# Second layer's attention: folded weights, a scale on GpSimd, heads summed in PSUM, unrolled by tiles

## What is computed

```
scores[h] = (X Wq[h] + bq[h]) (X Wk[h] + bk[h])^T / sqrt(128)
p[h]      = softmax(scores[h])
h         = h + sum over heads of p[h] (X Wv[h] + bv[h]) Wo[h]
```

## Time and profile before

| | us |
|---|---|
| median of three runs | 3473.49 |
| lowest, highest | 3467.41, 3475.90 |
| profiled execution, its own time | 3499.97 |
| its span | 3498.2 |

### The profile page before, as it was taken

One profiled execution on the slowest core, in us unless ns is written; L12 is line 12 of the kernel. 1 busy time (PEld: TensorE's weight loads), 2 busy tenths in 40 slices (PEclk: granted clock), 3 DMA queues, 4 the chain that ended last, 5 costly groups with the idle time before them and its releaser, 6 DMA issues.

```text
span 3498.2 us, 57433 instructions
## 1 busy us (share of the span) xinstructions
PE 3053.3 (87%) x18996; PEld 2673.3 (76%) x19032; DVE 2413.0 (69%) x4368; ACT 1801.3 (51%) x3135; POOL 1773.0 (51%) x1524
## 2 busy tenths in 40 slices
PE   1556666668999999879999999999799999999997
PEld 1434445457788888759999999999699999999986
DVE  1456766643677676657777777777577777777774
ACT  0256666523666565525555555555455555555544
POOL 5466656500200000126666666666366666666663
PEclk9879999969999999979999999999899999999997
DMA  1010000000000000010000000000000000000010
GB/s 41 32 25 18 19 13 18 7 25 21 13 0 0 0 0 0 11 50 28 27 27 27 27 27 27 27 27 28 17 28 27 27 27 27 27 27 27 27 34 7
DMA packets 36972, 75.92 MB, mean 22 GB/s; under 512 B 9644, under 2 KB 13876, under 8 KB 36120
## 3 DMA queue, kind: packets, MB, share of 16 engines
q1 hardware_dynamic: 35352, 71.68, 6.5%
q0 software_dynamic: 1536, 3.15, 0.3%
HBM read 65.36 MB, written 1.05 MB: 19 GB/s over the span
## 4 chain that ended last, share of the span: by engine, by line
PE 47%; issue 5%; POOL 3%; DVE 1%; ACT 0%; POOLq 0%; DVEq 0%; ACTq 0%
PE lat_ps_h L1837 19%; PE lat_ps_z L1851 9%; PE lat_ps_s L1763 7%; PE lat_ps_t L1790 6%; PE lat_ps_z L1781 3%; POOL lat_zz L1570 2%; PE lat_ps_z L1773 2%; PE lat_ps_z L1861 1%; POOL latm_wq L1549 0%; POOL latm_wq L1543 0%; POOL latm_att L1562 0%; POOL latm_vcg L1554 0%; PE lat_ps_s L1879 0%; DVE latm_norm L1669 0%; DVE latm_h L1675 0%
## 5 line engine op out<-in xcount | busy, mean ns | idle before, releaser
L1837 PE MATMUL lat_ps_h<-latm_share,latm_attT 100*128 100x256 f32 x6144 | 886.8, 286 | 0.1
L1837 PEld LDWEIGHTS lat_ps_h<-latm_share,latm_attT 100*128 100x128 f32 x6144 | 818.7, 189 | 24.9 <-DVE latm_attT L1626 11.8
L1562 POOL TENSOR_TENSOR latm_att<-latm_sc,latm_tot 128x400 f32<-128x400 f32 x516 | 441.3, 855 | 617.7 <-DVE latm_tot L1621 588.1
L1570 POOL TENSOR_TENSOR lat_zz<-lat_zz,lat_zsq 128x512 f32<-128x512 f32 x514 | 660.3, 1285 | 0.3
L1698 ACT ACTIVATE latm_sc<-latm_sc 128x400 f32<-128x400 f32 x516 | 279.1, 541 | 430.8 <-DVE latm_sc L1612 430.8
L1851 PE MATMUL lat_ps_z<-latm_attT,latm_vg 100*128 100x512 f32 x1536 | 485.8, 424 | 0.0
L1619 DVE TENSOR_REDUCE latm_tot<-latm_sc 128x4 f32<-128x400 f32 x516 | 291.3, 565 | 157.4 <-ACT latm_sc L1698 157.4
L533 POOL TENSOR_TENSOR ret_probs<-ret_probs,ret_shared 128x1024 f32<-128x1024 f32 x128 | 305.7, 2389 | 181.4 <-ACT ret_probs L666 181.4
L1626 DVE TENSOR_TENSOR latm_attT<-lat_ps_t,latm_attT 100x512 fp32r<-100x512 f32 x514 | 349.8, 681 | 61.7 <-ACT latm_attT L1714 61.7
L1714 ACT CAST latm_attT<-lat_ps_t 100x512 fp32r<-100x512 f32 x514 | 301.0, 586 | 147.3 <-PE lat_ps_t L1790 123.1
L1763 PE MATMUL lat_ps_s<-latm_wk,lat_xr 128*128 128x400 f32 x1548 | 368.8, 347 | 3.0 <-issue 3.0
(11 more groups left out here) (339 smaller groups left out, 5012.4 us busy)
## 6 DMA issues: line engine op xcount, KB each, us to landing
lat_w_in<-in_w_quads SPq DMA_DIRECT2D x65, 512.0 KB, 3.6
lat_wq_in<-in_wq_quads SPq DMA_DIRECT2D x65, 256.0 KB, 2.6
ret_qk_head<-ret_qk_parts SPq DMA_DIRECT2D x256, 32.0 KB, 2.0
moe_w<-in_W SPq DMA_DIRECT2D x2, 1024.0 KB
mha_wqk<-in_Wqk SPq DMA_DIRECT2D x1, 1152.0 KB, 5.6
ret_shared<-in_xpos_q SPq DMA_DIRECT2D x1, 1024.0 KB, 5.3
ret_shared<-in_xpos_k SPq DMA_DIRECT2D x1, 1024.0 KB, 5.0
latw_wkv<-in_Wkv SPq DMA_DIRECT2D x1, 1024.0 KB
```

The source lines that it names most:

```text
L1562: nc.gpsimd.tensor_tensor(att[:, u].rearrange("p (j l) -> p j l", j=QH), sc[:, u].rearrange("p (j l) -> p j l", j=QH), tot[:, u].unsqueeze ...
L1570: nc.gpsimd.tensor_tensor(zz[:, t], zz[:, t], zsq[:, u], ALU.add).then_inc(s["zz_added"], 1)
L1837: mm = e.matmul(ps_h[:, t, :], attT[:, t % 2, a_part, j * P:(j + 1) * P], share[:, u, w_part, j * FF2:(j + 1) * FF2], start=False, stop=Fa ...
```

## The change

Before the loop, the two weights of a head are multiplied once (`fold`): Wq[h] Wk[h]^T as `wqk` and Wv[h] Wo[h] as `wvo`, each 128 x 128 for a head. `keys` of a unit are then X times `wqk` plus a bias column `bqk`, and the scores are X itself (`xr`, already split) against `keys`: no q is made. The values are X times `wvo` plus `bvo`, so that p times them is already the head's share of the output, and `output` goes.

To take the biases in, POOL and DVE centre the query and key weights over the model width, with a bias column added, and X carries +1 (`lift`). These steps stand in front of and inside the norm (`means`, `fold`, `fold_bias`).

The heads of one sequence now come one after the other (n = 8 * sequence + head), and `gather` adds all 8 heads into the same two banks of `psO`; once for each sequence and half the sum is copied, turned back and added to h. Since heads are summed there, the division must come before: DVE's `invert` makes 1/sum of each tile (128x1), and GpSimd multiplies the tile's 128x1024 probabilities by it (`normed`), after the exponential and ahead of the transposes.

All is written out in 128 steps, one a tile, with no hardware loop. On PE every step holds the same parts: 6 matmuls of `gather` for tile step-7 on, 8 transposes of tile step-2, 6 matmuls of the scores of tile step+2, and in two steps of eight 3 matmuls of the next keys, in two others 4 of the next values, both into `psT[:, 0]`. `probs` has four buffers instead of three.

The weight transfers are seven instead of five, 2.0 MB in all instead of 2.8 MB.

```diff
@@ -103,9 +103,12 @@
-    def __init__(self, core, h, ident, xT, psT, l2=False, xr=None, room=None):
+    def __init__(self, core, h, ident, xT, psT, l2=False, xr=None, room=None, lift=None):
...
+        if meanwhile is not None:
+            meanwhile()
...
+                nc.scalar.activation(self.xr[:, 0, g * BANK:(g + 1) * BANK], src, ACT.Identity, bias=self.rise[:]).then_inc(self.high, 1)
...
@@ -947,244 +866,345 @@
+        makes_keys = lambda step: (step // TB + 1, step % TB // 2 - 1) if step < K - TB and step % TB in (2, 4) else None
+        makes_values = lambda step: ((step + 2) // TB, (step + 2) % TB // 2) if TB <= step + 2 < K and (step + 2) % TB in (0, 2) else None
...
-            with e.Fori(0, H) as hh:
-                for b in range(B):
-                    n = hh * B + b
-                    if b == 1:
-                        e.wait_ge(k_ready, START + n + 1)
-                        head_weights(hh + 1)
-                    low_values(n + 1)
+            nc.gpsimd.tensor_copy(bv_wide[:], bv[:].unsqueeze(2).to_broadcast([P, H, P])).then_inc(s["bv_widened"], 1)
+            e.wait_ge(s["qk_mean"], START + 2)
+            nc.gpsimd.tensor_tensor(wqT[:], wqT[:], wide(mean[:, 0]), ALU.add).then_inc(s["q_centred"], 1)
+            nc.gpsimd.tensor_tensor(wkT[:], wkT[:], wide(mean[:, 1]), ALU.add).then_inc(s["k_centred"], 1)
+            def low_values(n, half):
+                e.wait_ge(s["v_high"], START + 2 * n + half + 1)
+                nc.gpsimd.tensor_tensor(v[:, n % 2, 1, chunk(half)], v_full[:, chunk(half)], v[:, n % 2, 0, chunk(half)].bitcast(F32),
+                                        ALU.subtract).then_inc(s["v_ready"], 1)
+            low_values(0, 0)
+            low_values(0, 1)
+            for step in range(K):
+                e.wait_ge(s["inv_ready"], START + step + 1)
+                nc.gpsimd.tensor_scalar(probs[:, step % 4], probs[:, step % 4], inv[:, step % TB:step % TB + 1], None, ALU.mult
+                                        ).then_inc(s["normed"], 1)
+                if step >= 1 and makes_values(step - 1):
+                    low_values(*makes_values(step - 1))
...
+            def fold():
+                e.wait_ge(s["q_centred"], START + 1)
+                e.wait_ge(s["bv_widened"], START + 1)
+                for j in range(H):
+                    mm = e.matmul(psO[:, j // 4, j % 4 * D:(j % 4 + 1) * D], bv_wide[:, j], wo[:, j], start=True, stop=True)
+                mm.then_inc(s["folded"], 1)
+                for j in range(H):
+                    mm = e.matmul(psS[:, 1, j // 4, j % 4 * D:(j % 4 + 1) * D], wvT[:, j], wo[:, j], start=True, stop=True)
+                mm.then_inc(s["folded"], 1)
+                e.wait_ge(s["k_centred"], START + 1)
+                for j in range(H):
+                    mm = e.matmul(psS[:, 0, j // 4, j % 4 * D:(j % 4 + 1) * D], wkT[:, j], wqT[:, j], start=True, stop=True)
+                mm.then_inc(s["folded"], 1)
+            def fold_bias():
+                e.wait_ge(norm.xT_ready, START + NT // 4)
+                for j in range(H):
+                    mm = e.matmul(psT[:, 0, j:j + 1], wqT[:, j], bk[:, j:j + 1], start=True, stop=True)
+                mm.then_inc(s["folded"], 1)
+            def make_keys(n, c, dst):
+                for j, (w_part, x_part) in enumerate(PARTS):
+                    mm = e.matmul(dst, wqk[:, w_part, head_of(n % H)], xr[:, x_part, n // H * S + c * BANK:n // H * S + (c + 1) * BANK],
+                                  start=(j == 0), stop=(j == 2))
+                mm.then_inc(s["keys_made"], 1)
+            def make_values(n, half, dst):
+                for j in range(4):
+                    t = n // H * TB + 4 * half + j
+                    mm = e.matmul(dst[:, j * D:(j + 1) * D], xT[:, t * P:(t + 1) * P], wvo[:, head_of(n % H)], start=True, stop=True)
+                mm.then_inc(s["v_made"], 1)
...
+            def turn(k):
+                e.wait_ge(s["normed"], START + k + 1)
...
+                for t in (2 * q, 2 * q + 1):
+                    for v_part, p_part in PARTS:
+                        mm = e.matmul(psO[:, c, :], v[:, n % 2, v_part, t * D:(t + 1) * D], probsT[:, p_part, t, chunk(c)],
+                                      start=(hh == 0 and t == 0 and (v_part, p_part) == PARTS[0]),
+                                      stop=(hh == H - 1 and t == TB - 1 and (v_part, p_part) == PARTS[2]), skip_group_check=True)
...
-                    e.wait_ge(v_full_ready, START + n + 1)
-                    at.rest(e, n, products, v, ident[:], start=True, psO_free=values_ready, after_turn=next_unit)
-                    values(hh1, b1)
-                    first_scores(n + 1)
-                    output(hh, n, 0)
-                    output(hh, n, 1)
+                if LAG <= step < K + LAG:
+                    gather(step)
+                if step >= 1 and makes_keys(step - 1):
+                    n, c = makes_keys(step - 1)
+                    e.wait_ge(s["keys_ready"], START + 2 * n + c + 1)
+                if step >= 1 and makes_values(step - 1):
+                    n, half = makes_values(step - 1)
+                    e.wait_ge(s["v_full_ready"], START + 2 * n + half + 1)
+                for b, c in adds_out(step - 1):
+                    e.wait_ge(s["out_added"], START + 2 * b + c + 1)
+                if 2 <= step <= K + 1:
+                    turn(step - 2)
+                if step + 2 < K:
+                    score(step + 2)
+                if makes_keys(step):
+                    n, c = makes_keys(step)
+                    e.wait_ge(s["low_ready0"], START + max(0, step - 1))
+                    make_keys(n, c, psT[:, 0, :])
+                if makes_values(step):
+                    n, half = makes_values(step)
+                    e.wait_ge(s["low_ready0"], START + max(0, step - 1))
+                    make_values(n, half, psT[:, 0, :])
+                for b, c in adds_out(step):
+                    e.wait_ge(s["low_ready0"], START + min(K, step - 1))
+                    turn_out(b, c)
...
-                            add = e.scalar_tensor_tensor(hv, at.psO[:, half, j * P:(j + 1) * P], inv[:, t:t + 1], hv,
-                                                         ALU.mult, ALU.add)
+                e.tensor_reduce(mean[:, 0], wqT[:], AX.X, ALU.add).then_inc(s["qk_summed"], 1)
+                e.tensor_reduce(mean[:, 1], wkT[:], AX.X, ALU.add).then_inc(s["qk_summed"], 1)
...
+            def invert(k):
+                e.wait_ge(s["exped"], START + k + 1)
+                if k >= TB:
+                    e.wait_ge(s["normed"], START + k - TB + 1)
+                e.reciprocal(inv[:, k % TB:k % TB + 1], total[:, k % TB:k % TB + 1]).then_inc(s["inv_ready"], 1)
...
+                if step + 1 < K:
+                    maxima(step + 1)
+                if 2 <= step <= K + 1:
+                    low(step - 2)
+                if step < K:
+                    invert(step)
+                if makes_keys(step):
+                    low_keys(*makes_keys(step), psT[:, 0, :])
+                if makes_values(step):
+                    full_values(*makes_values(step), psT[:, 0, :])
+                for b, c in adds_out(step):
+                    add_out(b, c)
```

More of the change, by code:

```diff
@@ L974, in attention @@
-        SCALE = float(D) ** -0.5
+        psS = m.ps("psS", [P, 2, 2, BANK])
+        psT = m.ps("psT", [P, 2, BANK])
+        psO = m.ps("psO", [P, 2, BANK])
+        probs = m.sb("probs", [P, 4, S])
+        room = probs[:].rearrange("p a s -> p (a s)")
+        xr = m.sb("xr", [P, 2, NT * P], F32R)
+        norm = Norm(m, h, ident, xT, psT, xr=xr, lift=1.0,
+                    room=[room[:, i * NT * D:(i + 1) * NT * D].rearrange("p (t d) -> p t d", t=NT) for i in range(2)])
+        probsT = m.sb("probsT", [P, 2, TB, S], F32R)
@@ L1055, in _, with turn_out @@
+            def turn_out(b, c):
+                e.wait_ge(s["out_kept"], START + 2 * b + c + 1)
+                for j in range(4):
+                    mm = e.transpose(psT[:, 0, j * P:(j + 1) * P], outT[:, c * BANK + j * P:c * BANK + (j + 1) * P], ident[:])
+                mm.then_inc(s["out_turned"], 1)
+            fold()
             norm.tensor(e)
-            e.wait_ge(norm.xT_ready, START + NT // 4)
+            fold_bias()
             e.wait_ge(norm.xr_ready, START + NT // 4)
-            e.wait_ge(weights_in, 80)
@@ L1059, in _ @@
[L1059 to L1087 removed]
+            e.wait_ge(s["wqk_ready"], START + 1)
@@ new lines, in _ @@
+            e.wait_ge(s["wvo_ready"], START + 1)
+            for c in range(2):
+                make_keys(0, c, psS[:, 0, c, :])
+            e.wait_ge(s["bvo_ready"], START + 1)
+            for half in range(2):
+                make_values(0, half, psO[:, half, :])
+            e.wait_ge(s["bqk_ready"], START + 1)
+            e.wait_ge(s["keys_ready"], START + 2)
+            score(0)
+            score(1)
+            for step in range(K + 14):
```

(38 more changed lines are left out.)

391 lines of the change are left out of this document (142 added, 249 removed).

## The result

The changed kernel takes 3454.73 us (median of 6 runs, 3450.55 to 3457.79), the kernel before, run beside it, 3468.7 us (6 runs, 3463.42 to 3475.9): a ratio of 0.9957 with a 95% interval of 0.9942 to 0.9972. It is faster, by 14 us where 40 were forecast. The profiled execution took 3450.77 us.

A forecast was written before the change was run, and what follows sets the result against it. PE was taken to bound the attention (busy 572.75 of 578.00 us). First scores to end, 534.4 against 586.8, gives -52.4; the start +12; sum -40.4 off the median 3473.49: 3433 us. Range 3415 to 3466, 70% for 3415 to 3450.

The forecast's parts named there:

- The unit: Attention loop: PE's work for one unit of 8 steps takes 33.2 us with hand-overs, against 36.7 before.
- hand-overs: Attention loop: ACT and DVE emptying psT behind key matmuls costs PE 0.15 us on each of 28, 4.2 in all.
- GpSimd's scale: Attention step: multiplying 128x1024 probabilities by a column on POOL takes 3.0 us, bounds 2.39 and 4.13.
- the chain through the new wait: Attention loop: POOL's scale ends at 7.1 us, its transposes are wanted at 8.8; 1.7 us are left, costing nothing.
- The start: Attention before the first scores: centring, fold, norm, first keys and values make them 12 us later, bounds +8 and +16.
- Filling and draining: Attention loop's ends: the first step with a gather begins at 24.2 us; draining takes 19.0; first scores to end 534.4.
- The attention in sum: Whole attention stage: 52.4 us less from first scores to end, 12 more at the start, together -40.4.
- The following stage starts as before: Latent stage behind the attention: starts from h and a cold PE as before, with no term in the sum.
- cold fill: Rival, attention's filling: PE at 0.50 clock makes it 38 us instead of 24, start 3 more: +17, 3450 us; 10%.
- GpSimd as the bound: Rival, attention loop: a scale of 4.13 us makes POOL the bound, 3491 us, break-even at 3.99; 6%.
- The ring: Rival, attention loop: exponential, scores, transposes and copies in sequence take 4.5 us a step, 42 more: 3475; 5%.
- The hand-overs did not wait for ACT: Rival, attention's keys: finding ACT in an exponential costs each hand-over 1.1 us more, 31 in all: 3464; 8%.

The follow-up runs named there:

- twice_keys: slot16 with PE making each half of the keys of the 15 later units twice: 3496.05 us, ratio 0.9995 to the kernel before.
- again128: slot16 with a second GpSimd operation, on 128 columns of the scaled probabilities, in each of the 128 attention steps: 3434.07 us.
- before_pad115: The kernel before with 115 one-column memsets on VectorE at the program's start: 3497.08 us, ratio 1.0077 to the kernel before.
- slot16: The changed kernel with VectorE's latent loop over the quads entered at slot 16 of a 256-instruction fetch block: 3432.49 us, ratio 0.9893 to the kernel before.
- again512: slot16 with a second GpSimd operation, on 512 columns of the scaled probabilities, in each attention step: 3536.08 us.
- slot16_b: The kernel before with VectorE's latent loop over the quads entered at slot 16 of a fetch block: 3476.33 us, ratio 1.0014 to the kernel before.
- slot200: The changed kernel with VectorE's latent loop over the quads entered at slot 200 of a fetch block: 3435.13 us.
- hint: The changed kernel with a branch-prefetch hint at the head of VectorE's latent loop over the quads, its place left as it was: 3434.7 us.

## Why the prediction was wrong, step by step

- **The unit, right.** 33.2 us forecast, 33.2 measured; the step 3.72 and 3.71; PE busy 99% at full clock; hand-overs 0.15 and 0.18. twice_keys shows that PE's time is the unit's time.
- **GpSimd's scale, right.** 3.0 us forecast from the rows of 1493 and 3081 ns, 2.85 measured, the inverse 0.15 against 0.19. The room that I gave the chain through the new wait is there: again128 took 0.53 us of the 1.7 and left the time as it was.
- **The start, nearly right.** +12 forecast; the first scores come 36.3 us after the first load where they came 23.4, +12.9. The fold began as described, behind the centring, and ended 21 us behind the first load, as forecast. The first keys and values were mis-sized: 5.6 us for 3.1, at a granted clock of 0.53 (868.6 to 874.2); POOL's centrings, 1.9 us each for 2.4, gave some of it back.
- **Filling and draining, a little short.** 537.7 us from the first scores (874.23) to the last addition's end (1411.95) against 534.4, with 586.8 before. In the filling the key hand-overs have no gather to cover them and cost 1.56 each; the first gather came at +24.75 for the +24.2 I had. The draining took 20.9 for 19.0.
- **The attention in sum.** -36.0 measured for -40.4. This 4.4 us is the mis-sizing of the terms above.
- **The step that failed: "The following stage starts as before".** It was costed at nothing, and no work was named that could hide a cost. It starts as before, but its loops don't run as before: +17.1 us, made of about 21 us of stalls on VectorE's back edges less one of PE's, 4.4, that went. The sum had no term for what a longer program does to loops behind it. In its place the runs showed that both kernels' loops lose time by where they stand: moved by 115 instructions, the old one's latent stage grew by 27.2 us (before_pad115), and placed, the new one's shrank by 20.7 (slot16). Neither a rival nor the range's reasons had it; that 3454.7 lies inside the range, near the "cold fill", is chance, since that case did not occur.
- **The rivals.** GpSimd as the bound: not at 2.85 us, and again512 shows it real from 4.3. The ring: PE waits nowhere in the loop for exponentials. The hand-overs did not wait for ACT. The filling was not cold: PE's first 12 products of scores took 3.05 us.
- With the placement put right (slot16) the kernel takes 3432.5 us where the prediction said 3433. Part of that agreement is luck: the attention gave 4 us less than forecast, and the kernel before lost some 5 us at PE's back edges that the changed one doesn't.

## What to carry to other kernels

Unrolling a stage is not local: it moves every loop behind it in the instruction stream, and such a loop may then wait for its instructions at each back edge, as VectorE's with a body of 262 instructions did here. Compare the stages that were *not* touched first, look for "issue" in front of the first instruction of a pass and for more packets on the instruction queues, and place the loop heads (or hint the back edge) before judging the change. A stage's own gain is then read from the engine that bounds it: here PE's removed products, one to one.

## What the runs showed of the hardware

- A back edge that misses its instructions stalls VectorE for 2.3 to 2.5 us in one program and 3.4 to 3.6 in another, TensorE for 1.5 to 3.3 us; each costs the stage 2.7 to 4.6 us. It came at all 7 back edges or, on TensorE, from some pass on to the last (the last alone in the kernel before, the last five in slot16_b, with the same program on TensorE).
- Where a loop stalls, its instructions are fetched again in every pass: 80 packets on VectorE's instruction queue in place of 48, 125 on TensorE's in place of 63.
- A stall at the entry of a loop (2.3 to 2.6 us) came with a branch over padding, at both of VectorE's loops in slot200 and slot16_b and at the second alone in slot16, and also without one, at the second in hint.
- The view's releaser can mislead there: the same stall was put down to "issue" in one kernel and to PE's scores in the other.
- GpSimd multiplies 128x1024 by a column in 2.85 us, 128x512 by a constant in 1.49 and 128x128 in 0.53.
- The embedding stage, mostly gathers, took 91 to 92 us in most profiles and 118 in both on one chip, which shifts the whole program by 26 to 27 us.
